# A spectral block kernel: each tile's inverse width transform moved to two tiles behind its block matmuls

## What is computed

```python
xn = _gn(x)                                   # per image, 32 groups of 12 channels
bias = xn @ bias_w.T + bias_b
xf = rfftn(xn in 4 blocks of 96, axes=(H, W), norm='ortho')
r1 = relu(_block_mul(xr, w1[0]) - _block_mul(xi, w1[1]) + b1[0])
i1 = relu(_block_mul(xr, w1[1]) + _block_mul(xi, w1[0]) + b1[1])
r2 = _block_mul(r1, w2[0]) - _block_mul(i1, w2[1]) + b2[0]
i2 = _block_mul(r2, w2[1]) + _block_mul(i1, w2[0]) + b2[1]
out = x + irfftn(complex(r2, i2), s=(H, W), norm='ortho') + bias
```

## Time and profile before

| | |
|---|---|
| median of 3 runs | 469.6 us (469.51 to 469.71) |
| profiled execution, its own time | 468.5 us |
| its span | 466.7 us |
| TensorE matmuls busy | 428.3 us, 92% of the span |
| VectorE busy | 336.4 us, 72% |
| ScalarE busy | 239.5 us, 51% |
| additions of x (L1009) | 64, 610 ns each |

### The profile page before, as it was taken

One profiled execution on the slowest core, in us unless ns is written; L12 is line 12 of the kernel. 1 busy time (PEld: TensorE's weight loads), 2 busy tenths in 40 slices (PEclk: granted clock), 3 DMA queues, 4 the chain that ended last, 5 costly groups with the idle time before them and its releaser, 6 DMA issues.

```text
span 466.7 us, 16876 instructions
## 1 busy us (share of the span) xinstructions
PE 428.3 (92%) x7304; PEld 388.3 (83%) x7304; DVE 336.4 (72%) x771; ACT 239.5 (51%) x567; POOL 24.1 (5%) x16
## 2 busy tenths in 40 slices
PE   4556629999999999999999999999999999999996
PEld 5455519989999889989999889989998899987894
DVE  3694998576876688577867688667867687668724
ACT  2641428525774368525764367525754377425620
POOL 0020870000000000000000000000000000000000
PEclk9679859999999999999999999999999999999999
DMA  7550000026001600035001700034001700030003
GB/s 217 164 185 1 1 0 3 3 88 220 1 3 39 239 34 1 5 115 193 1 4 37 268 6 1 16 139 156 3 4 37 271 2 4 15 158 2 4 4 136
DMA packets 11641, 32.44 MB, mean 70 GB/s; under 512 B 4196, under 2 KB 5904, under 8 KB 11568
## 3 DMA queue, kind: packets, MB, share of 16 engines
q1 hardware_dynamic: 11568, 31.36, 18.9%
HBM read 15.63 MB, written 12.58 MB: 60 GB/s over the span
## 4 chain that ended last, share of the span: by engine, by line
PE 85%; DVE 7%; issue 3%; ACT 2%; DMA 1%; POOL 0%; DVEq 0%; SPq 0%; POOLq 0%; ACTq 0%
PE bank L522 85%; DVE biasw L919 2%; DVE r L994 1%; DMA x_sb<-in_x 1%; DVE y L919 1%; ACT junk L806 1%; DVE o_sb L1009 0%; DVE rsum L987 0%; DVE z L919 0%; DVE extreme L1137 0%; ACT junk L809 0%; DVE extreme L1142 0%; ACT y L818 0%; DVE rho L919 0%; DVE b1s L1110 0%
## 5 line engine op out<-in xcount | busy, mean ns | idle before, releaser
L522 PE MATMUL bank<-biasw,y 128*64 128x384 f16 x1152 | 109.4, 335 | 0.0
L522 PEld LDWEIGHTS bank<-biasw,y 128*64 128x64 f16 x1152 | 93.5, 196 | 2.3 <-issue 1.0
L522 PEld LDWEIGHTS bank<-w2s,rho 96*64 96x64 f16 (+1 forms) x3072 | 81.4, 109 | 4.4 <-issue 2.5
L522 PE MATMUL bank<-w2s,rho 96*64 96x96 f16 (+1 forms) x3072 | 84.4, 207 | 0.0
L838 ACT ACTIVATE z<-bank 128x384 f16<-128x384 f32 x72 | 35.3, 490 | 56.2 <-PE bank L522 56.2
L823 ACT ACTIVATE g<-bank 128x384 f16<-128x384 f32 x64 | 31.0, 484 | 64.1 <-PE bank L522 64.1
L522 PE MATMUL bank<-w1R,y 128*128 128x192 f16 (+3 forms) x768 | 59.3, 228 | 4.8 <-ACT y L818 3.5
L522 PE MATMUL bank<-z,tab 128*128 128x384 f16 (+1 forms) x216 | 45.8, 336 | 17.1 <-DVE rsum L987 17.1
L522 PEld LDWEIGHTS bank<-tab,x_sb 128*128 128x128 f32 x384 | 51.1, 201 | 9.2 <-issue 6.0
L522 PE MATMUL bank<-tab,x_sb 128*128 128x128 f32 x384 | 52.7, 285 | 6.0 <-DMA x_sb<-in_x 5.9
L919 DVE SCALAR_TENSOR_TENSOR z<-bank,z 128x384 f16<-128x384 f32 x72 | 39.7, 557 | 25.7 <-ACT z L838 24.7
(11 more groups left out here) (103 smaller groups left out, 434.5 us busy)
## 6 DMA issues: line engine op xcount, KB each, us to landing
x_sb<-in_x SPq DMA_DIRECT2D x16, 768.0 KB, 6.8
out<-o_sb SPq DMA_DIRECT2D x14, 768.0 KB, 4.2
y<-y SPq DMA_DIRECT2D x24, 128.0 KB, 2.8
out<-o_sb SPq DMA_DIRECT2D x8, 192.0 KB, 1.9
tab<-in_tab SPq DMA_DIRECT2D x1, 642.0 KB, 4.8
o_sb<-in_bias_wt SPq DMA_DIRECT2D x4, 144.0 KB, 2.7
b1s<-in_b1h SPq DMA_DIRECT2D x1, 384.0 KB, 5.2
o_sb<-in_w SPq DMA_DIRECT2D x2, 144.0 KB
```

What stands on the lines that cost most here:

```text
L522: return nc.tensor.matmul(o, lhsT, rhs, start=start, stop=stop, **kw)
```

## The change

`EARLY` goes and `BEHIND = 2` comes. On TensorE `p6` of tile `gi - 2` runs right after `c2_rho` of tile `gi`, for `gi` from 2 to 7, and tiles 6 and 7 run at the end. On VectorE `add_x` of tile 0 stands before `scales` of the next image, and each further one behind the `g_low` two tiles on. The number of instructions on each engine and their operands stay the same.

```diff
-        EARLY = 3
+        BEHIND = 2
...
                 for gi in range(8):
                     if gi >= 3:
                         c2_bias(b, p, gi, more, first)
-                    if gi == 7:
-                        p6(b, range(EARLY))
                     c2_rho(b, gi, more, first)
+                    if gi >= BEHIND:
+                        p6(b, [gi - BEHIND])
                     if gi == 1 and more:
                         mean(b + 1)
                     if gi == 3 and more:
                         variance(b + 1)
-                p6(b, range(EARLY, TILES))
+                p6(b, range(TILES - BEHIND, TILES))
...
                 g_low(b, 2, more)
+                add_x(b, p, 0)
                 if more:
                     scales(b + 1)
                 g_low(b, 3, more)
+                add_x(b, p, 1)
                 for gi in range(4, 7):
                     if more:
                         y_low(b + 1, 1 - p, gi - 4)
                     g_low(b, gi, more)
-                for t in range(EARLY):
-                    add_x(b, p, t)
+                    add_x(b, p, gi - BEHIND)
                 g_low(b, 7, more)
-                for t in range(EARLY, TILES):
+                for t in range(TILES - 1 - BEHIND, TILES):
                     add_x(b, p, t)
```

## The result

The changed kernel takes 478.0 us (median of 4 runs, 477.2 to 478.6) against 469.6 before in the same session: ratio 1.018, 95% interval 1.0162 to 1.0198. It is slower by 8.4 us; 477.9 was forecast. Its profiled execution has a span of 475.8 us.

The account below looks back on a forecast made before the run. The prediction took TensorE to bound the kernel. Changes of form (5.3 us), lost cover (3.1) and the last image (-0.07) summed to 8.3 us, giving 477.9 us beside the median of 469.6, with a range of 474.0 to 481.0.

Parts of the forecast that it names:

- TensorE as the pace: Whole kernel: TensorE, busy for 92% of the span, sets the time; added instructions and waits there cost in full.
- The changes of form: Output stages: more switches between full-width and half-array matmuls, 0.64 us an image, 0.82 in the last, 5.3 in all.
- The lost cover: End of output stage: fewer tiles hide tile 7's evacuation; TensorE waits 0.44 us an image, 3.1 us for seven.
- T: Time mark in an output stage: the start of `p6` behind `c2_rho` of tile 7.
- The hand-over: Step from a VectorE end to the start of TensorE released by it, taken as 0.15 us.
- The last image: Last output stage: 0.98 us more `p6` ahead, last addition 1.05 us earlier, together -0.07 us; form counted apart at 0.82.
- The sum: Whole kernel: 5.3 + 3.1 - 0.07 = 8.3 us slower.
- Costed at nothing: Edits put at zero: additions between `g_low`s on VectorE, later variance and `y_low`, earlier first half of a store.
- The near tie of `c1` with tile 4's addition: Start of `c1`: the addition it waits for ends at 155.30, `c1` starts at 155.44; spreading wins at most 0.1 us.
- The full drain: Rival: each added change of form on TensorE lays bare 0.163 us, 8.2 us instead of 5.3, giving 480.8; chance 0.12.
- No change: Rival: short pieces' weights load in slack and tile 7's evacuation is quicker; only -0.07 stays, 469.5; chance 0.05.
- faster: Rival: the 0.30 us around `p6` is pile-up at the stage's end, which spreading removes; -1.0 us, 468.6; chance 0.03.

Follow-up runs that it names:

- e4_join: Kernel before, with `p6` of tiles 0 and 1 directly ahead of the variance and tiles 2 to 7 at the end, except last image: 468.7 us, ratio 0.9960.
- e6_join3: Kernel before, with `p6` of tiles 0 to 2 directly ahead of the variance and 3 to 7 at the end, except last image: 467.6 us, ratio 0.9958.
- e2_early5: Kernel before, with five instead of three tiles of `p6` ahead of `c2_rho` of tile 7, three instead of five behind: 473.0 us, ratio 1.0056.
- e1_behind3: Changed kernel, with `p6` three tiles behind instead of two, and tile 0's addition behind `g_low` of tile 3: 472.9 us, ratio 1.0052.
- e3_singles: Kernel before, with `p6` of tiles 0, 1, 2 singly behind `c2_rho` of tiles 4, 5, 6, and tiles 3 to 7 at the end: 473.3 us, ratio 1.0060.
- e5_halves: Changed kernel, order untouched, with each `p6` matmul split into two of 64 output columns: 469.5 us, ratio 0.9996.
- e8_before_halves: Kernel before, order untouched, with each `p6` matmul split into two of 64 output columns: 468.8 us, ratio 0.9972.

## Why the prediction was right

**TensorE as the pace: right.** The granted clock is 1.00 from 79 us to the end in both profiles, and from 86 us on TensorE waits only for `g_low` of tile 7 and, before and after alike, once for VectorE in the last image. What was added to TensorE was paid in full in every image.

**The changes of form: the mechanism right, the sum right partly by luck.** I had 0.64 us an image, and the runs showed two prices in it mis-sized and one saving left out. From `c2_rho` of tile 3 to `c1` the stage took 155.44 - 139.20 = 16.24 and takes 158.36 - 141.79 = 16.57; tile 0's piece ahead of that adds 0.59 and some 0.13 around it, together 1.05. Less the wait of 0.41 that leaves 0.64. But a change into full width costs 0.10, not 0.12: the 1.16 of tile 7's `c2_rho` was taken behind a full-width piece, and tile 2's, behind the means, takes 137.66 - 136.60 = 1.06 instead of 1.04 with no change at its end, so 0.02 belong to the change back ahead of it. A change back ahead of `c2_bias` costs 0.14, not 0.08, 0.10 of it in the tile and 0.04 in the bias product behind. I had taken the nearest row, that of `p6` ahead of `c2_rho`, and it was too cheap; that the slower weight loads of `c2_bias` make the difference is argued, not shown. The variance, which I had left at its old price, became 0.11 cheaper, its matmuls starting 0.43 us ahead of the bias product instead of 0.54. So the sum is (6 - 3) x 0.10 = 0.30 for the ways in where I had 0.40, 4 x 0.14 - 0.10 = 0.46 for the ways back where I had 0.24, and -0.11 for the variance where I had nothing: 0.65. Three errors cancelled. e4_join and e6_join3 show the same saving at the variance. By starts I had expected 1.16 into a tile and 0.57 for it, and they are 1.13 and 0.59. The rows of the kernel before behind the 1.06:

```profile
136.60 1.23 PE L522 MATMUL bank<-w2s,rho 99*64 99x96 f16 x48
137.66 1.70 PE L522 MATMUL bank<-biasw,y 128*64 128x384 f16 x18
```

**The lost cover: right, 0.41 for 0.44.** Tile 7 starts at T + 1.41 where I had 1.42, and e2_early5 shows the wait alone, 0.43. The list of waits has 0.3 for the longest, where I had said about 0.4 each: it counts from modelled ends. The hand-over is 0.15 us, from 157.18 + 0.55 to 157.88, as in the earlier trace rows. It is paid in full, as the period of e2_early5 shows.

**The last image: nearly.** From its `c1` to the end of the span it takes 475.8 - 423.60 = 52.20 us, where it took 466.7 - 415.37 = 51.33: 0.87 more against 0.82 - 0.07 = 0.75 in my sum. The tail is as worked out, T + 2.83 for 2.84; what is over lies ahead of T, 0.97 instead of 0.82, where the five changes back at 0.14 instead of 0.08 outweigh those into full width at 0.10 instead of 0.12.

**The sum.** 7 x 1.06 + 0.87 = 8.3 us, as forecast; the medians stand 8.4 apart. That it fits to 0.1 us is luck: the errors in the terms of form cancelled, and 0.12 too little for the last image stood against 7 x 0.03 too much for the wait. The spans stand 9.1 apart, since the profiled execution after was 0.8 us late already at the first image's means (84.89 against 84.08), where nothing had changed: that part is spread of the start, not the change.

**Costed at nothing, and free:** the additions between `g_low`s, the later variance, the earlier stores. No wait for `y` appears; the last `y_low` ends at 151.70 + 1.28 = 152.98, 5.4 us ahead of `c1`, where I had counted some 5. The near tie of `c1` with tile 4's addition gave nothing: e1_behind3 and e2_early5 have fewer additions there, and their last pieces and periods show no gain. e4_join, which pushes that addition later, shows the other side of the tie, 0.03 us.

**The rivals.** The full drain would have given 480.8. As a price of 0.163 at each change it is refuted: every way in costs 0.10, and e3_singles has 0.51 an image where four such changes give 0.65. It was closer than I thought, though: beside a halved tile the two changes of a lone one cost 0.31, and 2 x 0.163 is 0.33. What TensorE does in this time no run shows. No change and faster needed the rows around `p6` to be something other than form. e5_halves and e8_before_halves changed the form, and with it the number of matmuls of `p6`, with the order untouched, and took the price away.

## What to carry to other kernels

Before moving matmuls between others, look at the form that each uses the array in (the columns and rows in its row): a lone group of another form paid 0.24 us here beyond its 0.49 of work, and splitting it into the neighbours' form, with twice the matmuls, was free. Spreading the work at a stage's end over the stage takes the cover from the last item's evacuation, so leave at the end as much work as that chain is long (1.4 to 1.5 us here, three tiles). A steady period between like starts tells 0.01 us where whole runs tell 1.

## What the runs showed that I had not expected

The bias product takes 1.54 us directly behind the block product's 96-column matmuls and 1.46 behind a halved tile of 384 columns or behind another bias product, 0.08 less for the same 18 matmuls. A piece of four small float32 matmuls is 0.11 us cheaper inside a full-width piece than on its own (0.43 against 0.54). Halved, a tile takes 0.49 us for six matmuls, as long as for three at full width. The starts come in pairs, as in the bias product, with 0.16 us from pair to pair.
